# Splitting the B, C and step projection into rounded passes, and moving skip terms and step sums in the scan of a Mamba layer

## The reference

```
xz = layernorm(x) @ W_in;  x_inner, z = split(xz)          # 512 + 512 columns
x_conv = silu(causal_conv4(x_inner) + conv_b)
xp = x_conv @ W_x                                          # 33 columns: B (16), C (16), step (1)
delta = softplus(step);  A = -exp(A_log)
y = selective_scan(x_conv, A, B, C, delta) + x_conv * D_skip
x1 = layernorm(x + x + (y * silu(z)) @ W_out)
# then: retention cross attention on the context, then a mixture of experts (8 experts, top 2)
```

## Time and profile before

| | |
|---|---|
| median of 3 runs | 1917.61 us (1916.32 to 1921.56) |
| the profiled execution | 1918.45 us, span of its trace 1916.7 us |
| PE busy | 1763.7 us, 92% |
| DVE, ACT, POOL busy | 1075.5, 757.1, 709.6 us |
| mean granted PE clock | 0.963 of full |

### The profile page before, as it was taken

How to read it: one execution, slowest core, us unless ns; L and a number is a source line. 1 busy time by engine, 2 the same in 40 slices (tenths; PEclk the granted TensorE clock), 3 DMA queues, 4 the chain that set the end, 5 groups by cost and what they waited for, 6 DMA issues and landing times.

```text
span 1916.7 us, 33397 instructions
## 1 busy us (share of the span) xinstructions
PE 1763.7 (92%) x8984; PEld 1440.8 (75%) x8985; DVE 1075.5 (56%) x2536; ACT 757.1 (40%) x1355; POOL 709.6 (37%) x623
## 2 busy tenths in 40 slices
PE   6999987999947899999999998999999999999980
PEld 4666655888845778888888876888888888888870
DVE  6777767888825567666676773333333333333326
ACT  5777754666512332322323232332333333333326
POOL 1110005898822334534445352332332232232233
PEclk9999998999977899999999999999999999999995
DMA  4444465888624332122221244333333333333329
GB/s 135 171 170 170 170 225 155 244 263 251 234 78 147 101 104 91 69 73 90 79 90 68 76 156 122 54 52 53 52 53 53 51 54 54 51 54 52 52 36 353
DMA packets 137704, 220.63 MB, mean 115 GB/s; under 512 B 40544, under 2 KB 110368, under 8 KB 129328
## 3 DMA queue, kind: packets, MB, share of 16 engines
q1 hardware_dynamic: 112064, 184.44, 29.1%
q0 software_dynamic: 25584, 35.54, 10.8%
HBM read 122.79 MB, written 97.12 MB: 115 GB/s over the span
## 4 chain that ended last, share of the span: by engine, by line
PE 39%; DMA 11%; POOL 6%; issue 6%; DVE 4%; ACT 2%; SPq 1%; POOLq 0%; ACTq 0%; DVEq 0%
PE back_ps L2381 13%; DMA acc<-back_y,back_token 9%; PE back_ps L2401 8%; PE back_ps L2283 5%; POOL back_turned_qk L1663 4%; PE back_ps L2269 3%; POOL sorted L1651 3%; PE back_ps L2260 3%; PE back_ps L2390 2%; PE back_ps L2214 2%; ACT back_out L1816 2%; PE back_ps L2222 2%; DVE back_y L2136 1%; DMA back_c_raw<-in_ctx_T 1%; PE back_ps L2369 1%
## 5 line engine op out<-in xcount | busy, mean ns | idle before, releaser
L2381 PE MATMUL back_ps<-back_w_gu,back_xe_T 128*128 x1620 | 407.6, 400 | 0.3 <-issue 0.2
L1689 POOL DMA_INDIRECT acc<-back_y,back_token x135 | 210.1, 1556 | 499.4 <-DVE back_y L2136 456.0
L2381 PEld LDWEIGHTS back_ps<-back_w_gu,back_xe_T 128*128 128x128 f32 x1620 | 295.4, 189 | 58.7 <-issue 1.0
L2129 DVE TENSOR_TENSOR back_h<-back_silu,back_ps 128x512 f32<-128x512 f32 x135 | 92.7, 687 | 366.9 <-PE back_ps L2381 366.9
L2401 PE MATMUL back_ps<-back_w_down,back_he_T 128*128 x1080 | 255.6, 380 | 0.8 <-ACT back_he_T L1810 0.8
L2401 PEld LDWEIGHTS back_ps<-back_w_down,back_he_T 128*128 128x128 f32 x1080 | 195.1, 191 | 21.6 <-issue 1.0
L1147 PE MATMUL front_ps<-front_xn_T,front_w_in_parts 128*128 128x512 f32 x768 | 186.4, 399 | 5.2 <-issue 3.3
L1651 POOL DMA_INDIRECT sorted<-back_x,back_slot x128 | 133.7, 1044 | 134.8 <-DVE back_slot L1960 100.6
L1147 PEld LDWEIGHTS front_ps<-front_xn_T,front_w_in_parts 128*128 128x128 f32 x768 | 143.3, 190 | 48.3 <-issue 18.5
L993 DVE SCALAR_TENSOR_TENSOR front_conv<-front_ps,front_conv_wb,front_conv 128x508 f32<-128x508 f32 (+2 forms) x192 | 141.2, 742 | 63.3 <-ACT front_conv L829 58.8
L1810 ACT ACTIVATE back_he_T<-back_ps 128x512 f32<-128x512 f32 x135 | 80.7, 598 | 242.4 <-PE back_ps L2390 242.4
(11 more groups left out here) (222 smaller groups left out, 2892.7 us busy)
## 6 DMA issues: line engine op xcount, KB each, us to landing
back_xe<-sorted SPq DMA_DIRECT2D x135, 136.0 KB, 2.1
gate_T<-front_gate_T SPq DMA_DIRECT2D x16, 1024.0 KB, 4.7
xc_T<-front_xc_T SPq DMA_DIRECT2D x16, 1024.0 KB, 5.6
front_xc_in<-xc_T SPq DMA_DIRECT2D x16, 1024.0 KB, 5.4
front_gate_in<-gate_T SPq DMA_DIRECT2D x16, 1024.0 KB, 6.4
front_x_rows<-in_x SPq DMA_DIRECT2D x16, 512.0 KB, 5.4
front_c_rep<-c_parts SPq DMA_DIRECT2D x128, 64.0 KB, 4.5
front_rows_in<-in_x SPq DMA_DIRECT2D x16, 512.0 KB, 7.3
```

The source lines that it names most:

```text
L1689: pool.indirect_dma_start(out=d["acc"][:, :], out_offset=bass.IndirectOffsetOnAxis(ap=token[:, r:r + 1], axis=0), in_=y[:, r % 2], in_offs ...
L2381: op = nc.tensor.matmul(dst[:, r % 2], xe_T[:, r % 2, x_part, k], w_gu[:, bass.ds(e, 1), m, w_part, k], start=(n == 0), stop=(n == len(PAS ...
```

## The change

1. **Projection to B, C and step.** `w_x_parts` holds W_x rounded (columns 0 to 32) and its rest (columns 64 to 96). ACT rounds each chunk of the convolution's output (`round_xc`), POOL forms the rest (`rest_of_xc`), and PE multiplies both by `w_x_parts` in 2 F32R matmuls of 512 columns per chunk in place of one fp32 matmul. The two halves of the result are added by ACT's `evacuate_xp` and DVE's `join_xp`. The chunks' matmuls are spread between the `project` calls. POOL's rests stand in front of the power of the next but one group.
2. **Step sums.** `delta` is split in two parts, so `upto` and `after` become two F32R tiles each (16 ACT instructions a group in place of 8), and L1271 and L1276 become two F32R matmuls each.
3. **Skip terms.** DVE adds the first two skip terms ahead of the five-instruction chain and the other two behind it. The statistics of group k-2 stand between the first pair and the chain. POOL's order is changed to fit (gates in two pairs, `scale_segment` one step earlier in the program), ACT's `inner` exponential too.
4. **Entry of the scan.** The last group's step, its segments and the choice of the scan move a step or two.

SP's program is unchanged.

```diff
+            def rest_of_xc(g, u, j):
+                pool.wait_ge(xc_high_ready, KI * g + j + 1)
+                nc.gpsimd.tensor_tensor(xc_parts[:, j % 2, 1], xc_T[:, u, j], xc_parts[:, j % 2, 0].bitcast(F32),
+                                        ALU.subtract).then_inc(xc_low_ready, 1)
...
+                    if not is_at(g, 0):
+                        rest_of_xc(g - 1, 1 - u, KI - 1)
+                    rest_of_xc(g, u, 0)
+                    rest_of_xc(g, u, 1)
                     if not last:
-                        rstd_of(2 * pair + u + 2, u)
+                        rstd_of(g + 2, u)
+                    rest_of_xc(g, u, 2)
...
+            def round_xc(g, u, j):
+                act.wait_ge(xc_ready, KI * g + j + 1)
+                if not (is_at(g, 0) and j < 2):
+                    act.wait_ge(xp_part_done, KI * g + j - 1)
+                nc.scalar.activation(xc_parts[:, j % 2, 0], xc_T[:, u, j], ACT.Copy).then_inc(xc_high_ready, 1)
...
+            def join_xp(g, u):
+                dve.wait_ge(xp_low_ready, g + 1)
...
+                nc.vector.tensor_tensor(xp_T[:, u], ps_xp[0:XP], xp_low, ALU.add).then_inc(xp_T_ready, 1)
...
                     if not (last and u):
                         split(g + 1, 1 - u)
+                    if not is_at(g, 0):
+                        join_xp(g - 1, 1 - u)
                     if not last:
                         statistics(g + 2, u)
...
+            def project_xp(g, j):
+                pe.wait_ge(xc_low_ready, KI * g + j + 1)
+                if is_at(g, 0) and j == 0:
+                    pe.wait_ge(w_x_ready, 3)
+                elif j == 0:
                     pe.wait_ge(xp_T_ready, g)
...
+                for part in range(2):
+                    op = nc.tensor.matmul(ps_xp, w_x_parts[:, j], xc_parts[:, j % 2, part], start=(j == 0 and part == 0),
+                                          stop=(j == KI - 1 and part == 1))
+                op.then_inc(xp_part_done, 1)
...
                     project(g, u, 0)
+                    if not is_at(g, 0):
+                        project_xp(g - 1, 2)
                     project(g, u, 1)
                     if not (last and u):
                         turn(g + 1, 1 - u)
                     if not is_at(g, 0):
-                        project_xp(g - 1, 1 - u)
+                        project_xp(g - 1, 3)
                     project(g, u, 2)
-                    if not is_at(g, 0):
-                        turn_xp(g - 1, 1 - u)
-                    project(g, u, 3)
+                    project_xp(g, 0)
+                    project(g, u, 3, None if is_at(g, 0) else lambda: turn_xp(g - 1, 1 - u))
+                    project_xp(g, 1)
...
+                for part in range(2):
+                    for s in range(GS):
+                        step_size = delta_parts[:, part].bitcast(F32)[:, bass.ds(g * GS + s, 1)]
...
-                    for j in range(KI):
-                        dve.wait_ge(y_done, KI * k + j + 1)
-                        nc.vector.scalar_tensor_tensor(y_T[:, u, j], xc_in[:, u, j], d_skip[:, j:j + 1], ps_y[:, j % 2],
-                                                       ALU.mult, ALU.add).then_inc(skip_added, 1)
+                    add_skip(k, u, 0)
...
+                if there(k):
+                    add_skip(k, u, 2)
...
-                    nc.tensor.matmul(ps_late, masks[:, MASK_LATE], upto.rearrange("p s t -> p (s t)"), start=True,
-                                     stop=True).then_inc(late_done, 1)
+                    for part in range(2):
+                        op = nc.tensor.matmul(ps_late, mask_ends[:, 0], upto[:, part].rearrange("p s t -> p (s t)"),
+                                              start=(part == 0), stop=(part == 1))
+                    op.then_inc(late_done, 1)
```

More of the change, by code:

```diff
@@ L909, in _, with scale_x @@
             act.wait_ge(a_ready, 4)
-            evacuate_xp(GROUPS - 1, 1)
-            evacuate_xp_rows(GROUPS - 1)
-            act.wait_ge(xp_rows_ready, GROUPS)
-            softplus_exp(most, every)
+            evacuate_xp(GROUPS - 1)
+            def scale_x(g, u, first):
+                for s in (first, first + 1):
+                    act.wait_ge(x_turned, GS * g + s + 1)
+                    act.sem_inc(act_passed, 1)
+                    nc.scalar.activation(dx[:, u, s], ps_x[:, s % 2], ACT.Copy, scale=delta[:, bass.ds(g * GS + s, 1)]
+                                         ).then_inc(dx_ready, 1)
             def sums_of(g):
@@ L958, in step @@
                     segments(0, most)
-                if is_at(k, -1):
+                    evacuate_xp_rows(GROUPS - 1)
+                    act.wait_ge(xp_rows_ready, GROUPS)
+                    softplus_exp(most, every)
+                if there(k + 2):
+                    act.wait_ge(scaled, k + 3)
+                    nc.scalar.activation(inner, inner, ACT.Exp).then_inc(inner_exp, 1)
+                if is_at(k, 0):
                     segments(most, every)
@@ L1074, in _, with add_skip @@
             all_steps(0, most)
+            join_xp(GROUPS - 1, 1)
+            nc.vector.tensor_copy(mask_ends.rearrange("p w r -> p (w r)"), masks[:, MASK_LATE.start:MASK_EARLY.stop]
+                                  ).then_inc(mask_ends_ready, 1)
+            compare_rows()
             choose()
+            def add_skip(k, u, first):
+                for j in (first, first + 1):
+                    dve.wait_ge(y_done, KI * k + j + 1)
+                    nc.vector.scalar_tensor_tensor(y_T[:, u, j], xc_in[:, u, j], d_skip[:, j:j + 1], ps_y[:, j % 2],
+                                                   ALU.mult, ALU.add).then_inc(skip_added, 1)
             def step(k, u):
@@ L1149, in project @@
                     op.then_inc(done, 1)
[L1151 to L1152 removed]
+                    if between:
+                        between()
+                        between = None
+            def project_xp(g, j):
[3 more added lines that the diff above has]
+                elif j == 0:
                     pe.wait_ge(xp_T_ready, g)
[L1154 to L1157 removed]
+                for part in range(2):
+                    op = nc.tensor.matmul(ps_xp, w_x_parts[:, j], xc_parts[:, j % 2, part], start=(j == 0 and part == 0),
+                                          stop=(j == KI - 1 and part == 1))
+                op.then_inc(xp_part_done, 1)
             def turn_xp(g, u):
```

186 lines of the change are left out of this document (112 added, 74 removed).

## The result

| | before | changed |
|---|---|---|
| median of 8 runs each, us | 1917.34 (1915.32 to 1921.56) | 1929.74 (1924.21 to 1933.09) |
| profiled execution, us (span) | 1918.45 (1916.7) | 1933.09 (1931.3) |
| one group of the projection, us | 16.16 | 16.30 |
| one step of the scan, mean of 13, us | 14.94 | 15.85 |

The ratio is 1.0061, with a 95% interval of 1.0049 to 1.0073: slower by 0.6%, 12 us, and within 1 us of the forecast of 1929.0.

A forecast was written before the change was run, and what follows sets the result against it. PE was taken to bound projection and scan until other loops close. 1918.45 + 2 (projection) + 14 (scan) - 1 (entry) - 2.5 (end) = 1931, as median 1930, stated as 1929; 8-in-10 range 1911 to 1941.

The forecast's parts named there:

- PE's saving and who eats it: Projection: PE's saving is eaten by the loop through ACT and DVE, 16.3 us a group, +2 us over 15 groups.
- The four links named above: Projection group: chunk 0's silu at 5.1, affine evacuation at 6.6, join ending at 10.35, chunk 2's silu at 14.45 us.
- GpSimd and DVE in the projection: Projection rival: casts and subtractions wait for GpSimd's rest, 0.6 us more a group, 9 us, 1938; chance 0.12.
- The late load: Scan: xc_in lands 2.5 us late every second step; loop of two steps 30.7 us, with clock drops +14 us.
- the share of the clock: Scan: PE drops to 1.2 GHz after each 2.5 us pause, about 1.4 us lost; +14 us with drops, +5 without.
- A sign that I had given: Scan: PE's clock in the stretch 345 to 510 us falls under 0.95.
- my pair of pauses: Basis for the clock drop: a 2.07 us PE pause was followed by lower clocks, one of 1.38 us was not.
- The clock holds: Scan rival: load late but no clock drop, pauses 1.25 us a step, scan +5 us, 1921; chance 0.25.
- The entry: Entry of the scan: added operations, an earlier chain and the late load together give -1 us, within 4 either way.
- The end: End of the scan: PE's 2.07 us wait for a skip term shrinks, with the clock's recovery -2.5 us.

The follow-up runs named there:

- act_order: Changed kernel with ScalarE's rounding of chunk 0 behind the affine evacuation and its copy of projected rows ahead of chunk 3's bias tap; 1923.36 us, ratio 1.0023.
- all_mended: Changed kernel with earlier skip terms, two ScalarE moves, store ahead of loads, and PE's projected-row transposes and first projection reordered; 1901.47 us, ratio 0.9923.
- scan_alone: Changed kernel with the projection of before: one fp32 pass a chunk, no rounding, rests or join; 1920.35 us, ratio 1.0011.
- store_first: Changed kernel with SP's store of the group before ahead of the scan's first loads in the last two projection groups; 1928.99 us, ratio 1.0059.
- the two fillers: filler_4 and filler_8: changed kernel with idle PE transposes ahead of the next group's first transposes; 1923.46 and 1926.39 us.
- turn_later: Changed kernel with PE's first four transposes of the next group behind the second half of the products; 1917.92 us, ratio 0.9998.
- skips_ahead: Changed kernel with DVE's last two skip terms of a step put back ahead of the chain; 1914.48 us, ratio 0.9974.
- filler_4: Changed kernel with four idle identity transposes a step on PE, where it waits for the load of xc_in; 1923.46 us, ratio 1.0034.
- filler_8: Changed kernel with eight idle identity transposes a step on PE, where it waits for the load of xc_in; 1926.39 us, ratio 1.0054.

## Why the prediction was right, and where it was not

**PE's saving and who eats it.** Right. PE does 25 and 16 us less and the group takes 16.30. The four links named above came within 0.2 us; act_order shows by experiment that it is this loop, and all_mended that it opens further, to 15.41.

**GpSimd and DVE in the projection.** The rival had a true piece: the two casts take 1.29 us beside the rest of chunk 0, where the pair took 0.82 before. The loop absorbed most of it (10.54 for 10.35), and not the 0.6 us a group that the rival wanted.

**The late load.** Right in place and size: pauses of 2.2 to 2.6 us in every second step (one of 4.30, whose load took 7.3 us to land), a loop of 30.7 us (two undisturbed pairs took 30.85 and 30.68), +11.8 us against +14. The pattern is less fixed than I had argued: in the changed kernel, scan_alone and store_first the lateness comes in every second step, in act_order as some 1 us in nearly each, in the same loop. What was too high is the share of the clock: I had a drop behind each pause. Windows of 2 us behind the pauses of 4.30, 2.60 and 2.22 us, and within and behind that of 2.54:

```profile
362.00:364.00 2.00, 2.00 (x11) 2.00 (x10) 1.97 (x2) 0.84 (x2) 1.84 (x4) 0.50 0.91 311
...
397.00:399.00 2.00, 2.00 (x12) 2.00 (x11) 1.97 (x2) 2.00 (x8) 1.93 (x2) 0.53 0.97 410
...
427.00:429.00 2.00, 2.00 (x12) 2.00 (x11) 1.84 (x2) 1.21 (x2) 1.99 (x1) 0.50 1.09 286
...
458.00:460.00 2.00, 1.27 (x12) 1.27 (x13) 1.81 (x6) 0.43 (x1) 2.00 (x2) 1.00 1.18 182
460.00:462.00 2.00, 2.00 (x20) 2.00 (x19) 1.88 (x1) 2.00 (x7) 1.92 (x2) 1.00 1.08 370
```

Three pairs of steps fall to 1.2 GHz and take 34.1, 32.3 and 32.5 us; the pair with 2.54 us keeps 2.4 GHz and takes 30.85, though its pause is longer than the 2.22. So it isn't the pause's length alone, and what else decides is open. A drop costs some 1.6 us a pair (32.3 and 32.5 for 30.85), about the 1.4 that I had. The sum is then 5.3 for the loop, 4.8 for three drops and 1.9 for the one load that landed late: 12.0, with 11.8 measured. A sign that I had given failed with it: the clock in 345 to 510 is 0.97, where I had written under 0.95. And my pair of pauses was thin ground: the rows that I cited for the one of 1.38 us end with its own window (the trace has 1.00 in the windows up to 552). "The clock holds", the rival at 1921, is what the two fillers and act_order's scan show: two steps of 29.9 to 31.1 us with no drop. The fillers stand at 1923.5 and 1926.4, with the entry's loss in them.

The Trainium skill's fit (DMA: Bandwidth & Descriptors, "Anatomy of one DMA") would have made the load 4.4 us. The 16 loads of xc_in took 5.1, 5.4 and 7.3 us (least, median, most) in the changed kernel, so the page's estimate is too low here.

**The entry.** Here a term failed: I had -1 us, within 4 either way, and it is +4.4, outside those 4, in the profiled execution. I counted operations on ScalarE and DVE and took PE's tail as unchanged. What I passed over is that taking 1.7 us of fp32 work from PE, and making `project_xp` need the current group's chunk instead of the last group's, takes away the cover of a store wait that was already in the trace, 5.38 us of ScalarE's. With that wait gone, in store_first, the first outside product comes 0.9 us later behind the last group's transposes than before, where in the changed kernel it comes 7.8 later.

**The end.** PE's wait for the skip term shrank from 2.07 to 0.25 us, and the stretch is 3.5 us shorter where I had 2.5.

```profile
548.66 2.05 PE L1321 MATMUL front_ps<-front_products,front_dx 128*128 128x128 f32 x16 [0.25 <-DVE front_y_T L1159]
```

Of the profiled execution I expected 1931 and it took 1933.1; the terms' errors partly cancel (entry +5.4, scan -2.2, end -1.0). The median lies 3.4 us under that execution, where I had taken 2 off, and that brings it within 1 us. So the mechanisms were found, but a hit within 1 us is luck: errors of 5.4 and 2.2 us stood against each other, and the execution that was profiled happened to be the longest.

## What to carry to other kernels

When the bound engine is relieved, lay out the next loop instruction by instruction through the engines that hand work to each other; the price of the change is that loop's length, and act_order, turn_later and skips_ahead each show that a place in the order, not an amount of work, sets it. A release (here of a load's buffer) has a due time: moved behind a chain of 7 us it turned 1.1 us of slack into pauses of 2.2 to 2.6 us. And look in the trace for waits that cost nothing today, because something covers them: they come due when the cover goes, and removing one of them helps only if the queue behind it isn't full.

## What was not expected of the hardware

Idle work did not make the kernel slower. Four transposes a step whose result nobody reads took 5 us off, eight took 1 us off, which is no difference. In both profiles PE's steps stay at 2.4 GHz, with pauses up to 1.7 and 0.9 us. That this is why filler_4 is faster fits its profile, and isn't shown, since act_order's scan holds the clock without idle work, and filler_8 holds it without being faster.

The order of DVE's work changed what GpSimd did to it. L1182, the first product of the chain (L1184 in skips_ahead), has this least, median and most in ns, first in the changed kernel, then in skips_ahead:

```profile
L1182 DVE TENSOR_TENSOR front_inner<-front_inner,front_c_rep x13: 1214/2112/2355, 345.9 to 536.3; 128x1024 f32<-128x1024 f32 x13
```

```profile
L1184 DVE TENSOR_TENSOR front_inner<-front_inner,front_c_rep x13: 1216/1218/1516, 329.5 to 503.4; 128x1024 f32<-128x1024 f32 x13
```

In the changed kernel it starts beside GpSimd's gates, and a GpSimd instruction on 4 elements takes as long as DVE goes on:

```profile
378.52 2.50 POOL L810 TENSOR_TENSOR front_y_T<-front_y_T,front_gate_in 128x512 f32<-128x512 f32 x2
...
379.96 2.14 DVE L1182 TENSOR_TENSOR front_inner<-front_inner,front_c_rep 128x1024 f32<-128x1024 f32 x1
...
381.10 1.09 POOL L828 TENSOR_SCALAR front_rstd<-front_mean 128x4 f32<-128x4 f32 x1
```

DVE's 2.14 us are 1.22 and some 0.9, while the gates run on for 1.06 us beside it; L828 ends 0.09 us after DVE does. That fits an exclusive hold of the two engines' common port, as the Trainium skill (SBUF — State Buffer, "shared port pair") has it: one of the two holds it for a whole instruction, and the other waits. To the letter, 1.06 and 1.22 would make 2.28 us, 0.14 more than measured. The wait makes the chain 1 us longer (6.97 us from 379.96, against 5.99 from 388.34 in skips_ahead), and in the changed kernel the load stands behind that chain. Whether skips_ahead won anything by the shorter chain, beyond what the earlier load gave, was not tested.
